# Two attentions and two mixtures of experts on one core: gates spread by DMA, another opening, another order of turns, and split projections

## The chip, the cores and the metric

One core of one Trainium2 chip runs the whole program. The metric is the device time of one execution in microseconds (us). TensorE (PE) multiplies, with its weight loads (PEld) shown apart; VectorE (DVE), ScalarE (ACT) and GpSimd (POOL) do elementwise work; SyncE (SP) only issues DMAs here. DVE, ACT and TensorE reach PSUM, the eight banks of 128x512 floats in which TensorE leaves its products; POOL works on SBUF alone.

## The reference

The input is x, 16 sequences of 256 tokens with 128 features, float32. Four layers follow each other, each of the form x = x + layer(layernorm(x)):

```python
x = x + attn_a(layernorm(x))     # 16 heads of 8; q and k RMS-normed per head; softmax(q k / sqrt 8) v; Wproj, bias
x = x + ffn(layernorm(x))        # 8 experts, top 2 of a softmax gate; plus one shared expert
x = x + attn_b(layernorm(x))     # 16 score heads in 8 pairs, rotary q and k; softmax(2h) - lambda * softmax(2h+1); RMS norm; Wo
x = x + ffn(layernorm(x))        # the same weights again

# ffn, per token: s = softmax(gate(x)), the two largest e
#   out = sum_e  w2[e]( silu((s_e x) w1[e]) * ((s_e x) w3[e]) )  +  w2s( silu(x w1s) * (x w3s) )
```

The gate multiplies x ahead of the expert. So the kernel runs every expert on every token, with x times a gate that is zero where the expert isn't among the two.

## The kernel before

x stays in SBUF for the whole run (`g.x`). Each engine has one instruction stream, written out by `all_steps` (L1649): attention A (`attention_a`), feed-forward f, attention B (`attention_b`), feed-forward h (both `feed_forward`). Within a stream the order is that of the program; engines wait for each other by semaphores (`ev(...)`, `wait_ge`), and an engine that waits holds everything behind it.

**Attentions.** One turn per sequence, 16 turns, each with 16 heads h = 0 to 15 as its clock. The tables `STAGE_A`/`AT_A` and `STAGE_B`/`AT_B` say at which head of which turn a task of a sequence is issued: stage 2 at (7,) is head 7 of the turn two before its own; a number of 16 or more is the next turn. A sequence passes norm, x_turn (transposes into bank XB, L391/L865), a copy to `s_xt` (L488/L990), project (float32 matmuls of x^T with 128x384 weights, L397/L874), the q and k work on DVE and POOL, transposes of k and q through the one bank QK (L338/L769), scores (L354/L787), exp on ACT (L467/L955), values (L368/L819), then o_turn, a_turn, out-projection and residual (L612/L1145). q and k are stored as high and low float32r parts (`split`, `lo`). In A, a Newton iteration of twelve small POOL steps (L522) makes the reciprocal root for the RMS norm.
In B the softmax needs each row's maximum. `maxima` (L804) multiplies q (copied as `s_qp`, L985) with k once, DVE reduces it (L1088, 128x1024 to 128x4, negated) into a spare column of `s_qs`, and then `q_final` transposes q again with this column in it (L769) and ACT copies it to `s_qt` (L976) for the real scores. `s_var` (L1139) and `s_vare` (L1164) are small DVE instructions ahead of POOL's powers (L1045, L1068).

**Feed-forward.** One turn per chunk of 512 tokens, 8 turns, each with nine steps e: eight experts and the shared one (e = 8). At step e TensorE does `up` of expert e+1 (six 128x512 products, L1289 to L1291: three float32r products of high and low parts for w1, three for w3), `spread` of e+3 (L1285), and `down` of e (L1327). The gates of a chunk are computed one chunk ahead, at the steps in `FF` (for the first chunk, inside the last turn of the attention, at `FF_LEAD` steps placed at heads by `LEAD`): norm, x_turn, logits, `best` (maxima, indices, masks), pow on POOL (four pieces, L1444), `gates` (L1535 to L1548). They then reach all partitions through TensorE: `s_turn` transposes them (L1353), ACT copies them (`f_st`, L1414), and `spread` multiplies them with a 0/1 matrix (`g.select`) into the bank SB. DVE's `scale` (L1471) multiplies SB with x^T to `f_xe`, ACT rounds it to `f_xe_hi` (L1403), and the remainder `f_xe_lo` is made by POOL (L1434), or by DVE for the experts in `LOW_ON_DVE` (L1476). DVE's `hidden` (L1487) forms silu(.) times the other product. The order on DVE at step e is: low part of e+2, hidden of e+1, scale of e+3, then the gates' tasks.

**Opening and splits.** `opening` loads x in five parts on SP's queue and the weights on ACT's, and makes the statistics for the first norm. At turn 12 of A, ahead of head 0, DVE makes `w1_hi`, `w3_hi` and `select` (L639 to L641); at turns 13 and 14, ahead of head 0, POOL makes `w1_lo` and `w3_lo` (L503).

## Time and profile before

| | us |
|---|---|
| median of 3 runs | 990.37 (986.24 to 992.31) |
| profiled execution | 989.17, its span 987.4 |
| busy: PE, DVE, ACT, POOL | 874.8, 732.5, 578.9, 528.6 |
| first scores of A | 35.7 |
| first up of f | 255.2 |
| first exp of B | 491.9 |
| first up of h | 767.5 |
| mean granted TensorE clock | 0.973 of full speed |

The span runs from the first to the last instruction of the profiled execution. Busy is the time in which an engine has an instruction under way; a busy TensorE isn't one at its peak, since its matmuls are pipelined. The four firsts divide the span into the opening, A, f, B and h.

### The profile page before, as it was taken

The numbers are of one execution on the slowest core, as the hardware profiler recorded it, in microseconds if no ns is written. First come the engines' busy times: TensorE is split into PE (matmuls) and PEld (weight loads), VectorE is DVE, ScalarE is ACT, GpSimd is POOL, SyncE is SP. The second block draws the span as 40 slices with busy tenths as digits, with TensorE's granted clock in tenths as the row PEclk, the third lists the DMA queues.
The fourth block names the chain that finished last, engine by engine and source line by source line (L and its number), as shares of the span: only waits on it lengthen the run. The fifth ranks groups of instructions, "written<-read, shape, count | busy, mean of one in ns | idle before, by whom it ended". The sixth has DMA issues, their size and how long they took to land.

```text
span 987.4 us, 22246 instructions
## 1 busy us (share of the span) xinstructions
PE 874.8 (89%) x7264; PEld 621.0 (63%) x7264; DVE 732.5 (74%) x1978; ACT 578.9 (59%) x903; POOL 528.6 (54%) x610
## 2 busy tenths in 40 slices
PE   2799999888999999999788888888878799999998
PEld 0355555545688777788555555555545688888887
DVE  4677777766777777777678898989883577767775
ACT  1478778766444434444488888888875344444443
POOL 4666666663444455554436575757542644454551
PEclk9999999988999999999899999999997899999999
DMA  8000000000000000000000000000000000000000
GB/s 235 1 2 1 0 0 0 0 2 2 1 1 1 1 1 0 0 1 1 1 2 1 1 0 0 0 0 0 1 1 1 1 12 12 12 7 4 11 11 23
DMA packets 14607, 8.70 MB, mean 9 GB/s; under 512 B 1616, under 2 KB 14160, under 8 KB 14544
## 3 DMA queue, kind: packets, MB, share of 16 engines
q1 hardware_dynamic: 12960, 7.28, 2.6%
q10 hardware_dynamic: 1584, 0.62, 0.2%
q8 instruction: 35, 0.57, 0.2%
q14 instruction: 28, 0.23, 0.1%
HBM read 5.80 MB, written 2.10 MB: 8 GB/s over the span
## 4 chain that ended last, share of the span: by engine, by line
PE 21%; issue 13%; DVE 11%; POOL 7%; ACT 2%; DVEq 0%; POOLq 0%; ACTq 0%
DVE s_qs L1088 6%; PE psum L819 5%; PE psum L787 5%; POOL f_xe_lo L1434 3%; POOL f_p L1444 3%; PE psum L1327 2%; PE psum L769 2%; PE psum L1289 1%; DVE f_xe L1471 1%; PE psum L885 1%; PE psum L1291 1%; PE psum L1290 1%; PE psum L874 1%; PE psum L804 1%; ACT f_xe_hi L1403 1%
## 5 line engine op out<-in xcount | busy, mean ns | idle before, releaser
L1403 ACT ACTIVATE f_xe_hi<-f_xe 128x512 fp32r<-128x512 f32 x128 | 80.9, 632 | 204.6 <-DVE f_xe L1471 204.6
L1434 POOL TENSOR_TENSOR f_xe_lo<-f_xe,f_xe_hi 128x512 fp32r<-128x512 f32 x64 | 83.9, 1311 | 184.6 <-ACT f_xe_hi L1403 184.6
L1088 DVE TENSOR_REDUCE s_qs<-psum 128x4 fp32r<-128x1024 f32 x128 | 156.3, 1222 | 35.4 <-PE psum L804 34.6
L1327 PEld LDWEIGHTS psum<-w,f_h 128*128 128x128 f32 x1152 | 147.7, 191 | 8.8
L1327 PE MATMUL psum<-w,f_h 128*128 128x128 f32 x1152 | 153.0, 276 | 0.0
L467 ACT ACTIVATE s_probs<-psum 128x1024 f32<-128x1024 f32 x128 | 125.9, 1023 | 33.1 <-PE psum L354 32.7
L955 ACT ACTIVATE s_probs<-psum 128x1024 f32<-128x1024 f32 x128 | 131.3, 1026 | 19.5 <-PE psum L787 17.8
L1289 PE MATMUL psum<-f_xe_hi,w_hi 128*128 128x512 f32 x288 | 127.0, 441 | 7.6 <-POOL f_xe_lo L1434 7.0
L1487 DVE TENSOR_TENSOR f_h<-psum,f_g 128x512 f32<-128x512 f32 x144 | 99.2, 689 | 44.9 <-ACT f_g L1388 34.6
L1291 PE MATMUL psum<-f_xe_lo,w_hi 128*128 128x512 f32 x288 | 114.1, 396 | 0.0
L1290 PE MATMUL psum<-f_xe_hi,w_lo 128*128 128x512 f32 x288 | 113.5, 394 | 0.0
L1471 DVE TENSOR_TENSOR f_xe<-psum,f_xt 128x512 f32<-128x512 f32 x128 | 87.3, 682 | 25.0 <-PE psum L1285 25.0
L1388 ACT ACTIVATE f_g<-psum 128x512 f32<-128x512 f32 x144 | 84.9, 589 | 22.9 <-PE psum L1291 22.5
L1444 POOL TENSOR_TENSOR f_p<-euler,f_sh 128x8 f32<-128x8 f32 x56 | 90.1, 1637 | 1.7
L787 PE MATMUL psum<-s_qt,s_kt 32*128 32x256 f32 x512 | 66.2, 335 | 24.0 <-DVE s_qs L1088 17.3
L787 PEld LDWEIGHTS psum<-s_qt,s_kt 32*128 32x128 f32 x512 | 40.1, 189 | 65.5 <-DVE s_qs L1088 30.4
L1476 DVE TENSOR_TENSOR f_xe_lo<-f_xe,f_xe_hi 128x512 fp32r<-128x512 f32 x64 | 44.4, 694 | 41.4 <-ACT f_xe_hi L1403 41.4
L368 PE MATMUL psum<-s_probs,s_v 128*32 128x256 f32 x1024 | 72.9, 405 | 1.1 <-ACT s_probs L467 1.1
L819 PE MATMUL psum<-s_probs,s_v 128*32 128x256 f32 x1024 | 72.0, 401 | 0.1
L1289 PEld LDWEIGHTS psum<-f_xe_hi,w_hi 128*128 128x128 f32 x288 | 54.4, 189 | 23.9 <-POOL f_xe_lo L1434 10.3
L804 PE MATMUL psum<-s_kt,s_qp 24*128 24x256 f32 x512 | 65.4, 336 | 3.1 <-DVE s_qs L1088 2.1
L1291 PEld LDWEIGHTS psum<-f_xe_lo,w_hi 128*128 128x128 f32 x288 | 54.3, 189 | 12.8
(177 smaller groups left out, 1732.6 us busy)
## 6 DMA issues: line engine op xcount, KB each, us to landing
out<-x SPq DMA_DIRECT2D x8, 256.0 KB, 2.3
x<-in_x SPq DMA_DIRECT2D x3, 512.0 KB, 9.6
w<-in_w SPq DMA_DIRECT2D x3, 512.0 KB, 7.5
x<-in_x SPq DMA_DIRECT2D x2, 256.0 KB, 3.9
select_raw<-in_select SPq DMA_DIRECT2D x1, 512.0 KB, 4.8
rope_cos<-in_rope_cos SPq DMA_DIRECT2D x1, 256.0 KB, 3.9
rope_sin<-in_rope_sin SPq DMA_DIRECT2D x1, 256.0 KB, 4.6
wqkv_a<-in_Wqkv_aT ACTq DMA_DIRECT2D x1, 192.0 KB, 3.6
```

The lines of the kernel that those rows point to most:

```text
L467: act.activation(dst, src, ACT.Exp).then_inc(ex_sb.sem, 1)
L787: ins = pe.matmul(S[:, o:o + SEQ], kt[r:r + 32, k % 2, q, c * P:(c + 1) * P], qt[r:r + 32, k % 2, q, :], start=True, stop=True)
L819: ins = pe.matmul(PV[32 * j:32 * j + 32, :], v1[:, km % 2, c, h // 2, :], probs[:, h % 8, c, :], start=(c == 0), stop=(c == 1))
L955: act.activation(probs[:, 2 * (i % 4):2 * (i % 4) + 2, :, :].rearrange("p j c s -> p (j c s)"), S, ACT.Exp).then_inc(ex_sb.sem, 1)
L1088: dve.tensor_reduce(o[:, r:r + 2, 2 * p:2 * p + 2, 24:25].bitcast(F32R), room(km, i).rearrange("p (r j s) -> p r j s", r=2, j=2), AX.X, AL ...
L1289: pe.matmul(dst, w_hi, x_hi, start=True, stop=False)
L1290: pe.matmul(dst, w_lo, x_hi, start=False, stop=False)
L1291: return pe.matmul(dst, w_hi, x_lo, start=False, stop=True)
L1327: ins = pe.matmul(Y[k % 2][:, t * P:(t + 1) * P], g.f_h[:, q, t * P:(t + 1) * P], g.w2[:, e, :], start=(e == 0 and t == 0), stop=(e == NE ...
L1434: pool.tensor_tensor(xe_lo[:, ring(e), :], src, xe_hi[:, ring(e), :], ALU.subtract).then_inc(xe_lo_pool.sem, 1)
L1444: pool.tensor_tensor(g.f_p[:, i * w:(i + 1) * w], g.euler[:, 0:w], g.f_sh[:, i * w:(i + 1) * w], ALU.pow).then_inc(pw_sb.sem, 1)
L1487: dve.tensor_tensor(g.f_h[:, q, :], H3[q], g.f_g[:, q, :], ALU.mult).then_inc(h_sb.sem, 1)
```

## The change

It has five parts.

1. **Gates by DMA.** The spreading through TensorE is gone. DVE transposes the gates in 32x32 blocks (`f_sg`), SP writes them to a DRAM tensor and reads each expert's row back, broadcast over the 128 partitions, into one of four buffers `f_gt`. `scale` multiplies that buffer with x^T.
2. **The feed-forward's order.** The gates' tasks of a chunk are issued two chunks ahead and spread over more steps (`FF`); `LOW_ON_DVE` goes from (2, 5, 6, 7) to (2, 3); the shared expert's parts are made at step 2; `LEAD` places the first chunk's tasks one or two heads earlier.
3. **Projections.** In both attentions the float32 projection becomes three float32r products of high and low parts. ACT makes `x_hi`, DVE `x_lo` (task `xl`), and the weights are split once.
4. **Attention B.** q is transposed and copied once, for maxima and scores alike. The maxima go to a tensor of their own (`s_mxs`), TensorE transposes them to 16 rows (`max_turn`), ACT copies these, and a DMA on SP writes them into the spare rows of `s_qt`. Two small instructions move from DVE to POOL, some tasks move by a head.
5. **Opening and splits.** x is loaded in eight parts, of which SP issues four ahead of the weights' arrival; statistics, roots and sequence 1's tasks have other places (`EARLY_A`); sequences 0 and 1 use more banks; sequence 0's Newton steps run on DVE; the splits of w1 and w3 stand at heads 11 and 5 instead of ahead of head 0.

```diff
-PARTS = ((0, 4), (4, 8), (8, 16), (16, 24), (24, 32))
-STATISTICS = ((-3, 0), (-2, 11), (-1, 12), (0, 8), (0, 12))
-ROOTS = ((-3, 0), (-2, 15), (-1, 15), (0, 15), (1, 5))
+PARTS = tuple((t, t + 4) for t in range(0, NT, 4))
+LOADED = ((0, 1), (1, 1), (2, 2), (2, 2), (3, 4), (3, 4), (3, 4), (3, 4))
+STATISTICS = {(-3, 0): (0,), (-3, 12): (1,), (-1, 8): (2,), (-1, 12): (3,), (0, 4): (4,), (0, 11): (5,), (1, 4): (6,), (1, 9): (7,)}
+ROOTS = {(-3, 0): (0,), (-2, 5): (1,), (-1, 13): (2, 3), (0, 14): (4, 5), (1, 14): (6, 7)}
...
+            if i == 4:
+                sp.wait_ge(first_loaded, first_count)
+            sp.dma_start(g.x[:, lo:hi, :], x_view[:, lo:hi, :]).then_inc(x_loaded[LOADED[i][0]], 16)
...
+                act.wait_ge(first_loaded, first_count)
+                act.activation(g.wqkv_a_hi[:], g.wqkv_a[:], ACT.Copy).then_inc(w_split, 1)
...
+NEWTON_ON_DVE = 1
+EARLY_A = {(1, "norm", 0): (-3, 11), (1, "xt", 0): (-2, 5), (1, "xt_keep", 0): (-2, 8), (1, "xl", 0): (-2, 8), (1, "qkv", 0): (-2, 9),
+           (1, "qkv", 1): (-2, 10), (1, "square", 0): (-2, 12), (1, "sums", 0): (-1, 3), (1, "newton", 0): (-1, 4)}
...
+    def room(m, c):
+
+        return bank(3) if m < 2 and c == 1 else XB
+
+    def turned(m, i):
+
+        return bank((5, 0, 1, 2)[i]) if m == 0 else QK
...
-                pe.wait_ge(qkv_sb.sem, qkv_sb.upto(m, c))
-                pe.matmul(XB[:, 0:3 * P], xt[:, c * P:(c + 1) * P], wqkv[:],
-                          start=True, stop=True).then_inc(qkv_mm.sem, 1)
+                if km >= 2:
+                    pe.wait_ge(qkv_sb.sem, qkv_sb.upto(m, c))
+                dst, c = room(km, c)[:, 0:3 * P], slice(c * P, (c + 1) * P)
+                pe.matmul(dst, x_hi[:, c], w_hi[:], start=True, stop=False)
+                pe.matmul(dst, x_hi[:, c], w_lo[:], start=False, stop=False)
+                pe.matmul(dst, x_lo[:, c], w_hi[:], start=False, stop=True).then_inc(qkv_mm.sem, 1)
...
-            if k in (13, 14):
-
-                pool.wait_ge(g.late_loaded, g.late_count)
-                pool.wait_ge(w_hi_sb.sem, k - 12)
-                w, hi, lo = ((g.w1, g.w1_hi, g.w1_lo), (g.w3, g.w3_hi, g.w3_lo))[k - 13]
-                pool.tensor_tensor(lo[:], w[:], hi[:], ALU.subtract)
             for h in part:
+                if k in (13, 14) and h == 5:
+
+                    pool.wait_ge(w_hi_sb.sem, k - 12)
+                    if k == 13:
+                        pool.tensor_tensor(g.wqkv_b_lo[:], g.wqkv_b[:], g.wqkv_b_hi[:], ALU.subtract)
+                    w, hi, lo = ((g.w1, g.w1_hi, g.w1_lo), (g.w3, g.w3_hi, g.w3_lo))[k - 13]
+                    pool.tensor_tensor(lo[:], w[:], hi[:], ALU.subtract)
...
+                if k in (12, 13) and h == 11:
+
+                    dve.wait_ge(g.late_loaded, g.late_count)
+                    if k == 12:
+                        dve.tensor_scalar(g.wo[:], g.wo[:], 4 * (1.0 - LAMBDA_INIT), None, ALU.mult)
+                    if k == 12:
+                        dve.tensor_copy(g.wqkv_b_hi[:], g.wqkv_b[:])
+                    w, hi = ((g.w1, g.w1_hi), (g.w3, g.w3_hi))[k - 12]
+                    dve.tensor_copy(hi[:], w[:]).then_inc(w_hi_sb.sem, 1)
...
+                for off in due("xl", 0, h, k):
+
+                    m = n + off
+                    dve.wait_ge(xt_sb.sem, xt_sb.upto(m, 1))
+                    dve.tensor_tensor(x_lo[:], XB[:, 0:SEQ], x_hi[:], ALU.subtract).then_inc(xt_sb.sem, 1)
...
-    "pv": 5, "norm": (9,), "xt": (3,), "qkv": (6, 10), "rot": (13,), "sum": (0,), "split": (6, 1), "lo": (7, 2),
-    "kt": (8, 19), "qp": (11, 16), "max": tuple(range(14, 30, 2)), "qf": (7, 15), "v": (4,),
-    "otr": (2, 4), "tokens": (2, 4), "diff": (6,), "sq2": (6,), "mean": (7,), "pow": (8,), "head": (8,), "atr": (12,),
+    "pv": 5, "norm": (9,), "xt": (3,), "xl": (4,), "qkv": (6, 10), "rot": (13,), "sum": (0,), "split": (6, 1), "lo": (7, 2),
+    "kt": (7, 19), "qp": (11, 15), "max": tuple(range(14, 30, 2)), "mt": (8, 16), "v": (4,),
+    "otr": (3, 5), "tokens": (3, 5), "diff": (6,), "sq2": (6,), "mean": (7,), "pow": (8,), "head": (8,), "atr": (13,),
...
+            def max_turn(m, km, p):
 
                 pe.wait_ge(mx_sb.sem, mx_sb.upto(m, 4 * p + 4))
-                if p == 0:
+                if km + 1 < NSEQ:
+                    if p == 0:
+                        pe.wait_ge(kt_sb.sem, kt_sb.upto(m + 1, 1))
+                    else:
+                        pe.wait_ge(qp_sb.sem, qp_sb.upto(m + 1))
+                elif p == 0:
                     pe.wait_ge(kt_sb.sem, kt_sb.upto(m))
-                elif km + 1 < NSEQ:
-                    pe.wait_ge(qp_sb.sem, qp_sb.upto(m + 1, 1))
                 else:
-                    pe.wait_ge(qf_sb.sem, qf_sb.upto(m, 1))
-                turn(qs[:, km % 2], p).then_inc(qf_mm.sem, 1)
+                    pe.wait_ge(mt_sb.sem, mt_sb.upto(m, 1))
+                pe.transpose(QK[0:16, 0:P], mxs[:, km % 2, p].rearrange("p r j c -> p (r j c)"),
+                             g.identity[:]).then_inc(mt_mm.sem, 1)
...
+                        act.activation(mt[0:16, p, :], QK[0:16, 0:P], ACT.Copy).then_inc(mt_sb.sem, 1)
...
+                    pool.wait_ge(ms_sb.sem, ms_sb.upto(m))
+                    pool.tensor_tensor(g.s_var2[:], g.s_ms2[:], g.rms_eps[:], ALU.add).then_inc(var_sb.sem, 1)
...
+        for m in range(NSEQ):
+            n = Step(None, 0, m)
+            for p in range(2):
+                sp.wait_ge(mt_sb.sem, mt_sb.upto(n, p + 1))
+                sp.dma_start(qt[24:P:32, m % 2, 2 * p:2 * p + 2, :].rearrange("r j (c t) -> r (j c) t", c=2).bitcast(F32),
+                             mt[0:16, p, :].bitcast(F32)).then_inc(row_sb[p].sem, 16)
...
-LOW_ON_DVE = (2, 5, 6, 7)
+LOW_ON_DVE = (2, 3)
+LOW_ON_POOL = (0, 1, 4, 5, 8, 6, 7)
+HIGH_ORDER = (0, 1, 2, 3, 4, 5, 8, 6, 7)
...
-LEAD = {1: (0,), 3: (1,), 4: (2,), 6: (3,), 8: (4,), 9: (5,), 13: (6,), 15: (7,)}
+LEAD = {0: (0,), 2: (1,), 3: (2,), 5: (3,), 6: (4,), 7: (5,), 13: (6,), 15: (7,)}
...
-    "norm": 8, "x_turn": 0, "xt_sb": 0, "logits": 1, "best": 1, "pow": (2, 2, 2, 2), "gates": 5, "s_turn": 6,
-    "st_sb": 6, "residual": 0, "rstd": 0,
+    "norm": 4, "x_turn": 5, "xt_sb": 5, "logits": 6, "best": 7, "masks": 8, "pow": 7, "sums": 2, "gates": 3,
+    "residual": 5, "stats": 6, "rstd": 8, "shared": 2,
 }
-FF_LEAD = {"x_turn": 0, "xt_sb": 1, "logits": 2, "best": 2, "exp": 4, "gates": 5, "s_turn": 6, "st_sb": 6}
+FF_LEAD = {"x_turn": 0, "xt_sb": 1, "logits": 2, "best": 2, "masks": 2, "exp": 4, "sums": 5, "gates": 5}
...
-            def spread(m, km, e):
-
-                if e == 0:
-                    if km == 0:
-
-                        pe.wait_ge(before.turned.sem, before.turned.upto(last))
-                    pe.wait_ge(st_sb.sem, st_sb.upto(m))
-                    pe.wait_ge(xe_sb.sem, xe_sb.upto(m - 1))
-                else:
-                    pe.wait_ge(xe_sb.sem, xe_sb.upto(m, e))
-                pe.matmul(SB, g.select[:, e, :], st[:, km % 2, :],
-                          start=True, stop=True).then_inc(sb_mm.sem, 1)
...
-                dve.tensor_tensor(xe[:, e % 2, :], SB, xt[:, km % 2, :], ALU.mult).then_inc(xe_sb.sem, 1)
+                dve.tensor_tensor(xe[:, e % 2, :], gt[:, e % 4, :], xt[:, km % 2, :], ALU.mult).then_inc(xe_sb.sem, 1)
...
-                dve.wait_ge(st_mm.sem, st_mm.upto(n))
-                dve.tensor_copy(ssp[:, :, 0:E].bitcast(F32R), g.f_m[:, 0, :, :]).then_inc(hi_sb.sem, 1)
-                dve.wait_ge(hi_sb.sem, hi_sb.upto(n + 1))
-                dve.tensor_tensor(ssp[:, :, E:2 * E], g.f_m[:, 0, :, :], ssp[:, :, 0:E], ALU.subtract).then_inc(lo_sb.sem, 1)
+                dve.wait_ge(sc_sb.sem, sc_sb.upto(m))
+                dve.wait_ge(written.sem, written.upto(m - 1))
+                dve.transpose(g.f_sg[:], g.f_m[:, 0, :, :].rearrange("p t e -> p (t e)")).then_inc(sg_sb.sem, 1)
...
+        for m in range(NCH):
+            n = Step(None, 0, m)
+            sp.wait_ge(sg_sb.sem, sg_sb.upto(n))
+            sp.dma_start(g.gates[m % 2].rearrange("e (t b j) -> b (e t) j", t=4, b=4),
+                         g.f_sg[:]).then_inc(written.sem, 16)
+            sp.wait_ge(written.sem, written.upto(n))
+            for e in range(E):
+                if e >= 4 or m > 0:
+                    sp.wait_ge(xe_sb.sem, xe_sb.upto(n, e - 3) if e >= 4 else xe_sb.upto(n - 1, e + 5))
+                sp.dma_start(gt[:, e % 4, :], g.gates[m % 2, e].partition_broadcast(P)).then_inc(gt_sb[e % 4].sem, 16)
+                if not first and e == 3 and m >= 2:
+                    store(m - 2)
```

## Rows read from the trace of the kernel before

**Rows 1.** Windows (A, feed-forward, two B turns): us, busy PE PEld DVE ACT POOL, clock, DMA.

```profile
122.76:135.33 12.57, 12.11 (x140) 6.88 (x132) 9.56 (x32) 10.07 (x14) 8.52 (x18) 1.00 0.00 0
342.77:369.40 26.63, 25.22 (x147) 21.06 (x146) 20.17 (x64) 11.42 (x20) 14.00 (x10) 1.00 0.00 1
620.34:654.17 33.83, 30.00 (x345) 18.23 (x346) 30.54 (x59) 28.54 (x47) 21.54 (x21) 1.00 0.00 0
```

**Rows 2.** Waits of TensorE's weight loads, 314.5 to 447.7; total us, times, longest.

```profile
PEld psum L1353 <- DVE f_ss L1548: 6.2, 5, 1.3
PEld psum L1285 <- DVE f_xe L1471: 3.1, 5, 0.8
PEld psum L1289 <- POOL f_xe_lo L1434: 2.7, 5, 0.6
```

**Rows 3.** Timeline of one expert's step; start, duration (us), engine, line, what.

```profile
338.66 0.40 PE L1285 MATMUL psum<-f_st,select 128*128 128x512 f32 x1
338.89 1.05 PE L1327 MATMUL psum<-w,f_h 128*128 128x128 f32 x8
339.80 0.51 PE L1289 MATMUL psum<-f_xe_hi,w_hi 128*128 128x512 f32 x1
341.31 0.39 PE L1285 MATMUL psum<-f_st,select 128*128 128x512 f32 x1
342.18 0.68 DVE L1471 TENSOR_TENSOR f_xe<-psum,f_xt 128x512 f32<-128x512 f32 x1
343.60 1.29 POOL L1434 TENSOR_TENSOR f_xe_lo<-f_xe,f_xe_hi 128x512 fp32r<-128x512 f32 x1 [3.85 <-ACT f_xe_hi L1403]
```

**Rows 4.** Timeline, two-input instructions of DVE and POOL at once, feed-forward.

```profile
347.23 1.28 POOL L1434 TENSOR_TENSOR f_xe_lo<-f_xe,f_xe_hi 128x512 fp32r<-128x512 f32 x1 [0.92 <-ACT f_xe_hi L1403]
347.60 0.96 DVE L1520 TENSOR_TENSOR f_sh<-f_lg,f_top 128x32 f32<-128x32 f32 x1
348.64 6.44 POOL L1444 TENSOR_TENSOR f_p<-euler,f_sh 128x8 f32<-128x8 f32 x4
351.20 0.69 DVE L1476 TENSOR_TENSOR f_xe_lo<-f_xe,f_xe_hi 128x512 fp32r<-128x512 f32 x1 [0.70 <-ACT f_xe_hi L1403]
```

**Rows 5.** DMA issues; count, KB each, us from issue to landing.

```profile
out<-x SPq DMA_DIRECT2D x8, 256.0 KB, 2.3
bqkv<-in_bqkv ACTq DMA_DIRECT2D x1, 192.0 KB, 6.7
```

**Rows 6.** Timeline of attention B, two small DVE instructions.

```profile
601.19 0.47 DVE L1139 TENSOR_SCALAR s_var<-s_ms 128x16 f32<-128x16 f32 x1
606.55 1.28 POOL L1061 TENSOR_TENSOR s_rot<-s_qkv,rope_sin 128x512 f32<-128x512 f32 x1
606.72 1.13 DVE L1164 TENSOR_SCALAR s_vare<-s_mv 128x2 f32<-128x2 f32 x1
607.84 1.22 DVE L1088 TENSOR_REDUCE s_qs<-psum 128x4 fp32r<-128x1024 f32 x1
```

**Rows 7.** Timeline of attention A: a projection; two residuals; the weight split.

```profile
120.03 0.91 PE L397 MATMUL psum<-wqkv_a,s_xt 128*128 128x384 f32 x2
191.28 0.41 DVE L612 TENSOR_TENSOR x<-psum,x 128x256 f32 x1
223.48 0.41 DVE L612 TENSOR_TENSOR x<-psum,x 128x256 f32<-128x256 f32 x1
209.70 2.62 POOL L503 TENSOR_TENSOR w_lo<-w,w_hi 128x1152 fp32r<-128x1152 f32 x1
209.74 2.87 DVE L577 CAST s_qs<-s_qh 128x512 fp32r<-128x512 f32 x1
```

**Rows 8.** Timeline of the opening.

```profile
17.52 0.29 POOL L522 TENSOR_TENSOR s_yt<-s_y 128x64 f32<-128x64 f32 x1 [10.48 <-DVE s_y L594]
22.42 1.07 POOL L530 TENSOR_TENSOR s_qh<-s_qkv,s_y 128x512 f32<-128x512 f32 x1 [0.23 <-POOL s_y L522]
35.70 0.80 PE L354 MATMUL psum<-s_qt,s_kt 32*128 32x256 f32 x8 [1.18 <-DVE s_qt L668]
```

372 lines of the change are left out of this document (194 added, 178 removed).

## The prediction

> **What bounds the kernel now.** I read the views in the order of the work. The busy time per turn comes first [rows 1]: each row is a steady stretch, one turn of attention A (12.57 us), one of the feed-forward (26.63 us), two of attention B (33.83 us, 16.92 each). In the feed-forward TensorE is busy 25.22 of 26.63 us and DVE 20.17: TensorE is the bound, with some waits. In A it is 12.11 of 12.57. In B DVE (30.54 of 33.83) and TensorE (30.00) are equally full, so there the two hand work to each other and neither is the bound alone.
>
> Next the waits of TensorE's weight loads over five feed-forward turns [rows 2]: 6.2 us for `f_ss` (the transpose of the gates), 3.1 us for `f_xe` (the spreading matmul waits until DVE has emptied its bank), 2.7 us for POOL's `f_xe_lo`. That is 1.24, 0.62 and 0.54 us a turn. The first two belong to instructions that the change deletes.
>
> Then one expert's step in the timeline [rows 3]: spread at 338.66, down matmuls at 338.89, the next up matmuls at 339.80. The six up matmuls end with the next spread's start at 341.31. So a spread takes 0.23 us, a down 0.91 and an up 1.51; the later `f_xe` of 342.18 and `f_xe_lo` of 343.60 show a second ring, priced below.
>
> **The feed-forward, 16 turns.** Deleted from TensorE in each: 8 spreads x 0.23 = 1.83 us, and the gate transpose, four 128x128 matmuls, 0.46 us (half of the eight in a down). Their waits go too, 1.24 + 0.62. Were nothing late next, a turn would be 26.63 - 4.15 = 22.5 us.
> Something is late next: the ring that feeds x. From an up's start (339.80) DVE multiplies its product (hidden), then gates x for two experts later (342.18), ACT rounds it, POOL subtracts (343.60 + 1.29 = 344.89) [rows 3]. That is 5.09 us, about 5.15 with the signal, and the up two steps later needs it. Two of TensorE's new steps are only 2 x (1.51 + 0.91) = 4.8 us; the spreads covered the rest. POOL now makes six of the eight gated low parts in place of four (experts 0, 1, 4 to 7). Walking the nine steps with 2.40 us each, at least 5.15 from the up two before to every up that needs a POOL low part (a DVE low part is 0.6 shorter and binds nothing), and x_turn (0.46, as half a down) and the logits (0.91, eight small loads as a down) at steps 5 and 6, gives 24.1 us a turn. Without the ring it is 9 x 2.40 + 1.37 = 23.0, which is also what 25.22 busy less 2.29 leaves.
> DVE loses two low parts of 0.69 and two casts and gains one 32x32 transpose: about -1.6 us, from 20.17 to 18.6. But the gating product changes its operands from PSUM and SBUF to SBUF and SBUF. The rows show what that risks: at 347.60 a 128x32 tensor_tensor with both operands in SBUF takes 0.96 us, ending when POOL's pass (347.23 + 1.28) ends; at 351.20 one of 128x512 takes 0.69 us in the midst of POOL's four pow (348.64 + 6.44) [rows 4]. So POOL's subtraction holds DVE up and its pow does not. The new products start about 0.35 us before POOL's previous pass ends, at this step length; on five pairs that makes 24.7, if none of it is caught up. I take 24.2, nearer the ring alone since DVE may reorder its slack, a gain of 2.45 us x 16 = 39 us (first and last turns of a layer lose their gates' work too, some of it outside the turn). Bounds: 22.9 (no ring, 60 us) and 25.5 (18 us, most of a POOL pass waited for at each product).
> The Trainium skill, "SBUF — State Buffer", section "Who interferes with whom", says that a DVE instruction with two SBUF inputs contends with any GpSimd instruction that reads SBUF, the later one fully blocked. Read to the letter the pow blocks too; the 0.69 us inside the pow speaks against that much. By the rule the turn would be that of the second rival.
> New waits: the gates go by DMA to DRAM and back. The gates are ready three steps before the first product, 3 x 2.5 = 7.5 us. The nearest transfers land 2.3 us after issue (256 KB to DRAM) and 6.7 us (a 192 KB row spread over partitions, among many others) [rows 5]. Two transfers: 4.6 us at best, 13.4 at worst; I take 6, hidden. The other broadcasts have four buffers, so 10 us each, and SP has no other work but the stores. Queued behind a late one on DVE are hidden(8), the statistics and the next products. The pow of POOL (6.44) moves to where POOL has no low part for three steps; cover 7.3 us. Pieces of the statistics and masks only change their step: nothing, as DVE has 5 us free; if that cover goes, 2 us a turn.
>
> **Attention B, 16 turns.** Right before the max reduction of 607.84 [rows 6] DVE sits in `s_vare`, 1.13 us for 128x2, which ends with POOL's pass (606.55 + 1.28). It and `s_var` (0.47 at 601.19) go to POOL: DVE -1.6, +0.41 for the new low part of x (as the 0.41 of [rows 7]), net -1.2. TensorE loses eight transposes (0.91, as a down), gains two (0.23), and each projection falls from 0.91 [rows 7] to three products of 384 columns, 3 x 0.17 + 0.17 of tail = 0.69: together -1.1. ACT, busy in 28.54 of 33.83, loses two 128x512 copies and gains two small ones. The row DMAs have eight heads (8 us) before their use, against 2.3 to 6.7: hidden. Because DVE and TensorE alternate, only what lies between two reductions counts: I see 0.5 us at s_vare, about 0.45 at the others. 0.95 x 16 = 15 us. Bounds: nothing (the small steps fill up again with the new DVE step and the later o_turn) and 2.0 a turn, 32 us.
>
> **Attention A, 16 turns.** Projections -0.22 x 2. But DVE now makes x_lo at the head of the turn, after the statistics of the residual, and the first projection waits for it: +0.3. Net -0.1 x 16 = 2 us; bounds -5 and +3.
>
> **The weight splits.** The two turns from 191.28 to 223.48 take 32.20 us against 2 x 12.57: 7.06 too long, and the turn after meets the second POOL pass, another 3. The reason stands at 209.70: POOL's `w_lo` (2.62 us) starts and DVE's cast of 209.74 takes 2.87 us [rows 7], with TensorE empty behind it. The change puts the DVE casts at head 11, the POOL passes at head 5, ahead of the wait for the Newton seed (POOL is busy in 8.52 of 12.57 us [rows 1]), and drops select. One DVE copy (v) still meets them. I take 7 of the 10 us back; bounds 3 and 10.
>
> **The opening.** First scores are at 35.70. Newton on POOL runs from 17.52 to 22.2 [rows 8]: twelve steps of 0.39. On DVE a step of 128x256 takes 0.41 [rows 7]; for 128x64 I estimate 0.22: -2. The two projections no longer wait for each other's addition (-2), the four turns of sequence 0 have a bank each instead of one (-3.5), x is normalised before the weights land (-1), and sequence 1 is taken out of its way. Added: split of the weights, some 1.5 us, beside the transposes. Sum -9; bounds -5 and -12.
>
> **The hand-overs.** Gates for the first chunk take 6 us by DMA instead of a transpose, a copy and a spread (0.46, some 0.6 and 0.23, with the signals 2 us), but are asked for two heads (some 2 us) earlier and the last exps hold the first up in any case; a pow of 6.44 us earlier on POOL. +1; bounds -3 and +6.
>
> **Sum.** -39 - 15 - 2 - 7 - 9 + 1 = -71 us. The profiled execution took 989.17 us (span 987.4), which is 1.2 below the median of the three runs, 990.37; so 918 to 919. I say 919.
>
> **Rivals.**
> TensorE floor. The ring is slack because DVE gets ahead within the turn; turns of 22.9. For it: no wait on POOL's part exceeds 0.6 today [rows 2]. Against: such waits exist although spreads slow the pace. 919 - 21 = 898. Chance 0.17.
> DVE locked out. Every gating product waits for a POOL pass as the 0.96 us one did, 0.8 x 8 = 6.4 us on an engine with 18.6: 25 and more, a turn of about 26; FF gains 10 in place of 39: 948. For it: [rows 4]. Against: the pow row, and that the products start late in the pass. Chance 0.15.
> B does not move: its turn stays 16.92 as the ring re-forms; 934. Chance 0.07, inside the range.
> Slower: gates late. If write and broadcast take together over 9 us, DVE's first product, and behind it hidden(8), hold TensorE, microsecond for microsecond. At the worst end, 13.4 plus 2 us of issue and a queue of four broadcasts (2 us more), a turn is 24.2 + 8.4 = 32.6 and 14 such turns cost 118 us: 1037. It is slower than before from a chain of 14 us (71 / 14 = 5 us over 9). Against: 2.3 us for a whole 256 KB store. Chance 0.05.
> Nothing: the gains are given back to within 1%, 0.03 (by a mixture of the lower bounds: 18 + 0 - 3 + 3 + 5 - 6 = 17 us, 972).
>
> **Numbers.** The forecast itself (905 to 935) has 0.53. The range takes in the floor rival and the locked one, 892 to 948; outside are the late gates, nothing, and the ends of the two. A measurement of this kernel tells about 1% from no change. Faster 0.92, same 0.03, slower 0.05.
>
> **What would show it.** Right: no PE wait before the feed-forward's transpose of the gates, turns of 24.2, waits on `f_xe_lo` of 1 to 2 us a turn, gating products of 0.69 to 1.05 us; B turns near 16.0 with s_vare gone from DVE; A turns 12.5; first scores at 26 to 27; a turn 13 to 15 of A under 14 us. Wrong: products of over 1.3 us, DVE waiting for `f_gt`, B at 16.9, or the copies of v holding A for 3 us.

## The result: no gain, and the profile after

The changed kernel took 991.76 us (median of 20 runs), the kernel before 988.78 in the same comparison: ratio 1.0029, 95% interval 1.0015 to 1.0042. The forecast was 919. The profiled execution took 989.9 us with a span of 988.0 (before 989.17 and 987.4). The interval lies just above 1: the changed kernel is 0.3% slower, and all of the 71 us of forecast gain is absent.

Stage by stage, from the starts of the same instructions in both traces (A's and B's residuals, the hidden products of the two feed-forward layers f and h):

| stretch | before | after | change | forecast |
|---|---|---|---|---|
| start to A's first residual | 66.4 | 59.9 | -6.5 | -9 |
| (first scores at) | 35.70 | 32.26 | -3.4 | 26 to 27 |
| ten turns of A | 124.9 | 126.2 | +1.3 | -1 |
| three turns of A with the weight splits | 45.1 | 38.3 | -6.7 | -7 |
| A's 14th residual to f's first hidden | 21.5 | 24.1 | +2.5 | hand-overs +1 in all |
| seven turns of f | 189.6 | 191.7 | +2.1 | -17 |
| f's last turn to B's first residual | 76.8 | 82.8 | +6.0 | |
| eleven turns of B | 186.2 | 178.1 | -8.1 | -10 |
| B's 12th residual to h's first hidden | 59.5 | 66.2 | +6.7 | |
| h and the end | 217.4 | 220.7 | +3.3 | -20 |

(The forecast's 39 us of the feed-forward are spread over 16 turns here, its 15 of B over 16. A hand-over is the stretch in which one layer's last turn and the next layer's first overlap: three rows, from A's 14th residual, from f's last turn and from B's 12th residual.) Attention behaved; the feed-forward, expected to give 39, lost 5, and the hand-overs lost 15.

The busy time of steady stretches, as [rows 1]: two turns of A, one of f, two of B; columns as there, and GB/s last.

```profile
110.08:135.44 25.36, 23.67 (x269) 14.55 (x268) 18.91 (x65) 19.81 (x26) 17.15 (x37) 1.00 0.00 0
350.22:378.17 27.95, 23.80 (x138) 19.98 (x138) 21.33 (x63) 10.65 (x19) 16.83 (x13) 1.00 0.23 76
619.92:652.26 32.34, 28.22 (x336) 17.56 (x336) 29.21 (x57) 27.24 (x47) 22.16 (x25) 1.00 0.00 1
```

TensorE was in fact relieved in the feed-forward, from 25.22 us a turn [rows 1] to 23.80, and the turn is longer. So something else set its length. The waits of five turns of f, as [rows 2] (total, times, longest):

```profile
ACT f_xe_hi L1458 <- DVE f_xe L1520: 75.6, 40, 2.8
POOL f_xe_lo L1484 <- ACT f_xe_hi L1458: 55.8, 26, 3.8
DVE f_h L1536 <- ACT f_g L1443: 25.7, 21, 1.4
PEld psum L1361 <- POOL f_xe_lo L1484: 22.2, 24, 1.5
```

The waits for `f_ss` (6.2) and for the spread bank (3.1) are gone, and the wait for POOL's low part has gone from 2.7 to 22.2. One expert's step shows how the work runs in a circle, as [rows 3]:

```profile
361.70 0.68 DVE L1536 TENSOR_TENSOR f_h<-psum,f_g 128x512 f32<-128x512 f32 x1
362.31 0.68 DVE L1520 TENSOR_TENSOR f_xe<-f_gt,f_xt 128x512 f32<-128x512 f32 x1
363.10 0.63 ACT L1458 ACTIVATE f_xe_hi<-f_xe 128x512 fp32r<-128x512 f32 x1 [1.82 <-DVE f_xe L1520]
363.64 0.58 ACT L1443 ACTIVATE f_g<-psum 128x512 f32<-128x512 f32 x1
364.37 0.68 DVE L1536 TENSOR_TENSOR f_h<-psum,f_g 128x512 f32<-128x512 f32 x1
364.97 0.68 DVE L1520 TENSOR_TENSOR f_xe<-f_gt,f_xt 128x512 f32<-128x512 f32 x1
```

Gating product, its rounding, the silu queued behind the rounding on ACT, the hidden product, and on DVE behind it the next gating product: 362.31 to 364.97, 2.66 us, with no matmul in it (DVE also makes a low part in this step). The same circle ran before the change, 339.52 to the `f_xe` of 342.18 [rows 3], 2.66 us too; these are its lines between, which the prediction did not look at:

```profile
339.52 0.68 DVE L1471 TENSOR_TENSOR f_xe<-psum,f_xt 128x512 f32<-128x512 f32 x1
340.24 0.63 ACT L1403 ACTIVATE f_xe_hi<-f_xe 128x512 fp32r<-128x512 f32 x1 [1.47 <-DVE f_xe L1471]
340.81 0.60 ACT L1388 ACTIVATE f_g<-psum 128x512 f32<-128x512 f32 x1
341.57 0.69 DVE L1487 TENSOR_TENSOR f_h<-psum,f_g 128x512 f32<-128x512 f32 x1
```

Before the change 48 of 106 steps of steady turns, hidden product to hidden product, last 2.55 to 2.63 us, most of them 2.59; after it only 25 of 106 do, other short ones last 2.46 or 2.64. The long ones, up to 4.7 us, hold the places where DVE and POOL meet, as [rows 4]:

```profile
366.89 1.26 POOL L1484 TENSOR_TENSOR f_xe_lo<-f_xe,f_xe_hi 128x512 fp32r<-128x512 f32 x1
367.44 1.26 DVE L1520 TENSOR_TENSOR f_xe<-f_gt,f_xt 128x512 f32<-128x512 f32 x1
371.02 1.50 DVE L1520 TENSOR_TENSOR f_xe<-f_gt,f_xt 128x512 f32<-128x512 f32 x1
373.12 2.06 DVE L1548 TENSOR_SCALAR f_xn<-x,mean,rstd 128x128 f32 x4
373.26 1.33 POOL L1484 TENSOR_TENSOR f_xe_lo<-f_xe,f_xe_hi 128x512 fp32r<-128x512 f32 x1 [1.29 <-ACT f_xe_hi L1458]
374.64 0.50 PE L1361 MATMUL psum<-f_xe_hi,w_hi 128*128 128x512 f32 x1 [1.31 <-POOL f_xe_lo L1484]
```

Gating products of 1.26 and 1.50 us instead of 0.68, and a normalisation of 2.06 that takes 1.11 in the kernel before (337.50). The hidden product (375.10) stands behind the normalisation; TensorE's up of 374.64 waits for the low part of 373.26, which is late because the product of 371.02 is.

### The profile page after: what moved, and what is told of

Read it like the earlier page. It is cut to its first block, busy times and chain, and to the rows that moved or that the text cites. A ratio compares the mean times of both kernels' runs of the same rounds, so it can differ in the third digit from the quotient of the medians.

```text
span 988.0 us, 21977 instructions
## 1 busy us (share of the span) xinstructions
PE 834.2 (84%) x7040; PEld 600.9 (61%) x7040; DVE 724.2 (73%) x1949; ACT 556.2 (56%) x889; POOL 577.3 (58%) x668
## 4 chain that ended last, share of the span: by engine, by line
POOL 15%; PE 14%; DVE 13%; issue 9%; ACT 2%; POOLq 0%; DVEq 0%; ACTq 0%
DVE s_mxs L1156 7%; POOL f_xe_lo L1484 4%; POOL s_inv L1110 3%; POOL f_p L1496 2%; PE psum L874 2%; PE psum L842 2%; PE psum L1399 2%; PE psum L1361 2%; POOL s_qh L1084 1%; POOL s_rot L1125 1%; POOL s_rot L1126 1%; PE psum L1362 1%; PE psum L1363 1%; DVE f_xe L1520 1%; DVE s_qs L1183 1%
## 5 line engine op out<-in xcount | busy, mean ns | idle before, releaser
L1484 POOL TENSOR_TENSOR f_xe_lo<-f_xe,f_xe_hi 128x512 fp32r<-128x512 f32 x96 | 122.3, 1275 | 194.0 <-ACT f_xe_hi L1458 194.0
L1156 DVE TENSOR_REDUCE s_mxs<-psum 128x4 fp32r<-128x1024 f32 x128 | 155.9, 1219 | 29.1 <-PE psum L859 27.8
L1361 PE MATMUL psum<-f_xe_hi,w_hi 128*128 128x512 f32 x288 | 129.5, 450 | 51.4 <-POOL f_xe_lo L1484 46.9
L1399 PEld LDWEIGHTS psum<-w,f_h 128*128 128x128 f32 x1152 | 150.5, 193 | 10.9
L1520 DVE TENSOR_TENSOR f_xe<-f_gt,f_xt 128x512 f32<-128x512 f32 x128 | 103.9, 812 | 4.3 <-DMA f_gt<-gates 4.3
L1361 PEld LDWEIGHTS psum<-f_xe_hi,w_hi 128*128 128x128 f32 x288 | 54.8, 190 | 79.2 <-POOL f_xe_lo L1484 59.5
L842 PE MATMUL psum<-s_qt,s_kt 32*128 32x256 f32 x512 | 68.4, 345 | 37.6 <-DVE s_mxs L1156 35.2
L1496 POOL TENSOR_TENSOR f_p<-euler,f_sh 128x8 f32<-128x8 f32 x56 | 95.4, 1729 | 1.8
L874 PE MATMUL psum<-s_probs,s_v 128*32 128x256 f32 x1024 | 75.7, 417 | 0.0
L400 PE MATMUL psum<-s_probs,s_v 128*32 128x256 f32 x1024 | 72.1, 401 | 1.3 <-ACT s_probs L503 1.3
L859 PE MATMUL psum<-s_kt,s_qt 24*128 24x256 f32 x512 | 67.7, 343 | 3.6 <-DVE s_mxs L1156 2.7
L1362 PEld LDWEIGHTS psum<-f_xe_hi,w_lo 128*128 128x128 f32 x288 | 55.1, 191 | 6.5
```

Source lines behind the costliest of these rows:

```text
L842: ins = pe.matmul(S[:, o:o + SEQ], kt[r:r + 32, k % 2, q, c * P:(c + 1) * P], qt[r:r + 32, k % 2, q, :], start=True, stop=True)
L1156: dve.tensor_reduce(mxs[:, km % 2, p, r:r + 2, :, c:c + 1].bitcast(F32R), room(km, i).rearrange("p (r j s) -> p r j s", r=2, j=2), AX.X, A ...
L1361: pe.matmul(dst, w_hi, x_hi, start=True, stop=False)
L1362: pe.matmul(dst, w_lo, x_hi, start=False, stop=False)
L1399: ins = pe.matmul(Y[k % 2][:, t * P:(t + 1) * P], g.f_h[:, q, t * P:(t + 1) * P], g.w2[:, e, :], start=(e == 0 and t == 0), stop=(e == NE ...
L1484: pool.tensor_tensor(xe_lo[:, ring(e), :], src, xe_hi[:, ring(e), :], ALU.subtract).then_inc(xe_lo_pool.sem, 1)
```

## The experiments

Two theories on the feed-forward. **S (step ring):** the 2.59 us circle above sets the short steps, before and after, because of DVE's order; TensorE was not the bound. **L (lock):** POOL's subtraction shuts out DVE's instructions with both operands in SBUF, and some with one there (the normalisation above); the change made the gating product one of the first and gave POOL six gated low parts instead of four. Rivals: **C**, the chain of low parts through POOL is long by itself; and my own reading, TensorE. The table has the turn (mean of five in f, five in h, from one profiled execution each) and the whole kernel against the kernel before of the same chip. Excerpts of code leave out the semaphores' waits and marks.

| kernel | f turn | h turn | us | ratio (95%) |
|---|---|---|---|---|
| before | 27.22 | 26.64 | | |
| changed | 27.61 | 26.97 | 991.76 | 1.0029 (1.0015 to 1.0042) |
| e1, no subtraction on POOL | 25.44 | 24.78 | 969.46 | 0.982 (0.979 to 0.986) |
| e2, product ahead of hidden | 24.28 | 23.50 | 942.47 | 0.956 (0.952 to 0.959) |
| e3, x from PSUM | 26.62 | 26.39 | 979.90 | 0.993 (0.991 to 0.995) |
| e4, e2 + e3 | 23.49 | 22.44 | 926.28 | 0.937 (0.934 to 0.940) |
| e5, before with tiny spreads | 26.99 | 26.41 | 984.69 | 0.998 (0.996 to 1.001) |
| e6, before with e2's order | 25.56 | 25.55 | 972.88 | 0.984 (0.981 to 0.987) |
| e15, e1 + e2 | 24.30 | 23.21 | 940.45 | 0.952 (0.948 to 0.956) |

**e1.** The lock alone.

```diff
-pool.tensor_tensor(xe_lo[:, ring(e), :], src, xe_hi[:, ring(e), :], ALU.subtract)
+pool.tensor_tensor(xe_lo[:, ring(e), 0:6], g.euler[:, 0:6], g.minus_half[:, 0:6], ALU.pow)
...
+if k == 13: pool.memset(g.f_xe_lo[:].bitcast(F32), 0.0)      # once, in attention A
```

> Changed kernel, but GpSimd's low part in the feed-forward is a power of 128x6 elements (estimated from 1.00 us for 128x4 and 1.73 us for 128x8: 1.3 us) instead of the subtraction of 128x512 (1.28 us): the same wait, the same place, nearly the same time, but almost nothing read from SBUF. Left out: the low parts of the gated input. Theory L (lock): VectorE's gating product, with both operands in SBUF since the change, is shut out while GpSimd subtracts; then the products are all 0.69 us (now 0.69 to 1.50), and the feed-forward turn falls from 27.8/27.0 to 23.5 to 24.5 us, the kernel by 45 to 55 us to 935 to 945. Rival C (chain): the turn is long because six instead of four low parts go through GpSimd, 1.3 us each in the chain product, high, low, up; then the turn stays within 0.5 us of 27.8/27.0 and the kernel at 980 or above.

All 128 products took 0.68 to 0.72 us, though POOL was as busy (1.32 us for each stand-in). The turn fell by 2.2 us in both layers, not by 3 to 4, and the kernel came to 969, above the 935 to 945 expected. L is real and C as the whole cause falls, but it gives back 20 to 22 us of the kernel, under a third of what was missing. Some 3 us of that comparison are the edit's own: the memset takes 2.23 us of POOL (204.98) in the three turns with the weight splits, which last 41.3 us against 38.3.

**e2.** The ring alone: one pair of lines of DVE's order.

```diff
+for m, km, next_e in ahead(n, k, e, 3):
+    if next_e < E: scale(m, km, next_e)
 for m, km, next_e in ahead(n, k, e, 1):
     hidden(m, km, next_e)
-for m, km, next_e in ahead(n, k, e, 3):
-    if next_e < E: scale(m, km, next_e)
```

> Changed kernel, VectorE's order in a feed-forward step turned round: the gating product for three steps ahead before the hidden product. Theory S (step ring): most steps, before and after the change, last 2.59 us because the silu on ScalarE stands behind the rounding of the next product, that waits for the product, that stands on VectorE behind the hidden product, that waits for the silu before: 0.69 + 0.63 + 0.58 + 0.69. Then the short steps fall from 2.59 to 2.3 to 2.45 us (TensorE's own work), and if the lock of theory L is what is left in the long ones, the turn goes from 27.8/27.0 to 25 to 26.5. Rival: the short steps are TensorE's own length; they stay at 2.59 and the turn stays or grows, since the hidden product comes later.

The turn fell by 3.3 and 3.5 us, more than expected, and the kernel by 4.4% against the one before, 4.7% against the changed one. Of the 106 steps only 4 still last 2.55 to 2.63 us; short ones are 2.0 to 2.5. Nothing was taken away from any engine, and the gating products are not shorter for it (0.85 us in the mean in f, 0.91 in h). So DVE's order is the cause of 3.3 to 3.5 us a turn. That the circle of 2.59 us is all that it does is not shown: after the change part of the gain lies in the step behind the longest one, 2.46 us before and 1.26 now, where TensorE seems to catch up on what it had waited for.

**e3 and e4.** The product's x from the PSUM bank that the spread had used, for six of eight turns in a layer (one ACT copy of 128x512 a turn); e4 has e2's order too.

```diff
+if 2 <= k + 1 < NCH and e == 5:
+    act.activation(X, xt[:, (k + 1) % 2, :], ACT.Copy).then_inc(xp_sb.sem, 1)
...
-dve.tensor_tensor(xe[:, e % 2, :], gt[:, e % 4, :], xt[:, km % 2, :], ALU.mult)
+dve.tensor_tensor(xe[:, e % 2, :], gt[:, e % 4, :], X if km >= 2 else xt[:, km % 2, :], ALU.mult)
```

> Changed kernel, with the transposed x for the gating products held in the PSUM bank that the change freed (one ScalarE copy of 128x512 a turn, some 0.6 us, for six of eight turns of a layer): the product reads SBUF and PSUM as it did before the change. Output complete. Theory L: the products are 0.68 us in these turns, the turn falls to 24.5 to 26 (the normalisation and two low parts on VectorE still meet GpSimd), the kernel to 955 to 970. Rival C: products shorten but the turn stays within 0.5 of 27.8/27.0.

> e3 and e2 together. If L and S both hold, the two causes are separate and their gains add: turns of 23 to 24.5 us, the kernel at 935 to 955. If only L holds: as e3. If neither: near 988.

In e3 the products of these turns are 0.67 to 0.68 us, and the turn is 1.0 and 0.6 us shorter, less than half of e1's gain. The rest of the lock is on DVE's small instructions, which e1 freed and e3 did not: in the mean an `f_xn` takes 0.52 us in the changed kernel and in e3, 0.35 in e1; `f_sh` 0.85, 0.85 and 0.17; `f_vare` 0.65, 0.65 and 0.17. DVE's own low parts take 0.69 in all three. e3 missed its range (980 against 955 to 970). e4 went beyond its own, turns of 23.49 and 22.44 against 23 to 24.5 and 926 us against 935 to 955, and took what e2 and e3 gave apart (4.3 and 4.1 us a turn summed, 4.1 and 4.5 together). Four of its turns in the view of busy time (PE, PEld, DVE, ACT, POOL):

```profile
794.55:883.15 88.60, 88.60 (x555) 78.46 (x554) 70.23 (x197) 46.62 (x80) 61.34 (x45) 1.00 0.33 108
```

TensorE is busy in 88.60 of 88.60 us, and neither its matmuls nor its weight loads stand in the list of waits of this stretch. Here it is the bound, as I had thought it was before the change: 22.15 us a turn is what its work comes to.

**e5 and e6.** The same question put to the kernel before, from both sides.

```diff
+w = CH if km == 0 else 32
-pe.matmul(SB, g.select[:, e, :], st[:, km % 2, :], start=True, stop=True)
+pe.matmul(SB[:, 0:w], g.select[:, e, :], st[:, km % 2, 0:w], start=True, stop=True)
```

> Kernel before, but the spreading matmul of every chunk after a layer's first writes 32 columns instead of 512: TensorE is relieved of some 0.2 us x 8 a turn and nothing else is touched (the gates of the rest of the columns are left out). The prediction held TensorE to be the feed-forward's bound (25.22 us busy of 26.63): then the turn falls by 1.5 to 1.8 us and the kernel by 20 to 25 us. Theory S (the step of 2.59 us is a ring of VectorE and ScalarE: product, high part, silu, hidden, and the next product) says that TensorE was not the bound: the turn falls by less than 0.5 us, the kernel by less than 8.

> Kernel before, with the gating product ahead of the hidden product in each step of VectorE's order, as in e2. Theory S: the ring is opened, and TensorE becomes the bound: 25.2 us of its work in a turn and some waits, so 25.5 to 26.3 instead of 26.7 us a turn, the kernel 6 to 18 us faster. If TensorE was the bound already: no change (within 4 us).

Relieving TensorE of its spreads moved the turn by 0.23 us in both layers and the kernel by less than it can be measured. In e5 the steps of 2.59 us stayed (47 of 106 in 2.55 to 2.63). Turning DVE's order round moved the turn by 1.7 and 1.1 us and left none of them, and only then did TensorE's spreads bind: DVE's idle time before the gating products that ended with the spreading matmul rose to 74.7 us over the kernel, from 25.0:

```profile
  PE psum L1285: 25.0, 15
```

```profile
  PE psum L1285: 74.7, 84
```

(Kernel before, then e6: total us, times.) Both came out as theory S had it. This is the plainest answer to the prediction: the spreads, the largest part of what the change deletes, were not in the way.

**e15.** Both causes away.

> e1 and e2 together: GpSimd's low parts as a power of the same length that does not shut VectorE out, and the gating product ahead of the hidden one. Left out: the low parts of the gated input that GpSimd makes. With neither the lock nor the step ring, TensorE is left: 8 x 6 up and 32 + 4 down matmuls and the transposes and logits of the gates, as e4 shows in the second layer, so 22.1 us a turn there (26.97 in the changed kernel, 24.78 with the ring alone, 23.50 with the lock alone). Rival, a third limit in the low parts' chain through GpSimd (six of 1.3 us and 6.6 us of power a turn): above 23.

23.21 in h, not 22.1, and 24.30 in f, which is e2's 24.28: the rival's condition (above 23) is met, and the gains of e1 and e2 do not add. TensorE's weight loads wait for POOL's part again (4.6 us, four times, from 794 to 883), which in e4 they never do there. POOL's power for the gates took 1.87 us a piece in the median against 1.64 in e4, and its stand-in 1.35 in the mean against 1.29 for the subtraction there. The values are not the reason, for e2, with the real ones, has 1.91. Every piece over 1.7 us, in all kernels, ran while a DVE tensor_tensor with both operands in SBUF was under way: 48 of 56 pieces in e2, 11 in e4, none in the kernel before, whose product reads PSUM. So with x in SBUF the lock also works the other way: the product holds POOL's power up, by as much as 0.5 us, though the power does not hold the product up (52 products beside a power alone took 0.67 to 0.70 us in e2). POOL's chain is then the next limit, within 1 us of TensorE's. (e15 has e1's memset too, and 42.4 us in the turns with the weight splits against 38.3.)

**e8.** The gates' way over DRAM.

```diff
-sp.wait_ge(sg_sb.sem, sg_sb.upto(n))
-sp.dma_start(g.gates[m % 2].rearrange(...), g.f_sg[:]).then_inc(written.sem, 16)
-sp.wait_ge(written.sem, written.upto(n))
...
-sp.dma_start(gt[:, e % 4, :], g.gates[m % 2, e].partition_broadcast(P))
+sp.dma_start(gt[:, e % 4, :], g.row[e].partition_broadcast(P))
```

> Changed kernel with the broadcasts of the gates read from a constant table in DRAM, with no write of the gates and no wait for it (the gates are left out of the result; all of VectorE's work for them stays). It prices the latency of the gates' way. Theory: in the steady turns nothing waits for it (no wait on f_gt is seen), so 27.8/27.0 stays within 0.3; at the hand-overs VectorE waited 4.3 us for the first chunk's gates (753.69 to 758.03 in B's end), so 3 to 8 us come back in both together. Rival: the traffic itself (16 broadcasts of 256 KB a turn stay) or nothing: no change at all.

27.57 and 27.01 a turn, the kernel 991.67 (0.49% above the one before, 0.29% for the changed one): the latency costs nothing that shows. The wait of 4.3 us that DVE has in B's end is gone there, and the stretch from B's 12th residual is no shorter (67.0 us against 66.2). The stretch from A's 14th residual is shorter (20.8 us against 24.1), but no wait for the gates stood in it, and e8 has the full clock all through it, while the others with the same code there have 3.4 to 10.2 us at 1.2 GHz and take 22.1 to 24.1 us. Right about the turns, wrong about the hand-overs.

**e7.** The projections.

```diff
-pe.matmul(dst, x_hi[:, c], w_hi[:], start=True, stop=False)
-pe.matmul(dst, x_hi[:, c], w_lo[:], start=False, stop=False)
-pe.matmul(dst, x_lo[:, c], w_hi[:], start=False, stop=True)
+pe.matmul(dst, x_hi[:, c], w_hi[:], start=True, stop=True)      # x_hi, w_hi: the whole float32 here
```

> Changed kernel with both attentions' projections as one float32 product of x and the weights again (the low part of x is not made; the splits of the weights stay). The prediction gave -0.1 us a turn of A (12.4/12.95 now) and some 0.44 + 0.4 us of TensorE and VectorE a turn of B (16.17 now) to the three products. If that was right: B turns 16.3 to 16.6, A turns within 0.2. Rival: the low part of x on VectorE is a new wait (A: the first projection waits for it; the hand-over from the feed-forward to B: TensorE waited 4.29 us for it at 465.23): then A turns fall by 0.2 to 0.4 us, B does not grow, and the stretch from the feed-forward's turn 7 to B's first residual (82.8 us, 76.8 before) falls by 3 to 5 us.

The rival, nearly on every count. A's turn falls from 12.62 to 12.46 (0.2 to 0.4 was expected), B's from 16.20 to 16.11, and from f's last turn to B's first residual it takes 78.6 us instead of 82.8. The first scores come at 29.51 instead of 32.26, but A's first residual no earlier (59.8 against 59.9). The changed kernel's wait there:

```profile
464.75 0.42 DVE L1240 TENSOR_TENSOR s_x_lo<-psum,s_x_hi 128x256 fp32r<-128x256 f32 x1
465.23 0.44 PE L935 MATMUL psum<-wqkv_b_hi,s_x_hi 128*128 128x384 f32 x1 [4.29 <-DVE s_x_lo L1240]
466.06 0.49 ACT L1060 ACTIVATE s_qkv<-psum 128x384 f32<-128x384 f32 x1 [6.09 <-PE psum L937]
466.53 0.77 PE L1361 MATMUL psum<-f_xe_hi,w_hi 128*128 128x512 f32 x1
```

`s_x_lo` stands on DVE behind the layer's statistics and a cast that waits for POOL's rotation; the projection waits for it, and the feed-forward's next up matmuls stand behind the projection. But the kernel gained little (984.93, ratio 0.995, 0.992 to 0.999): it lost 2.1 us in the turns with the weight splits and 2.0 before h's first hidden product, where its clock was the lowest of all (next table).

**e9.** Attention B's last turns.

```diff
-turn(qs[:, km % 2], p).then_inc(qp_mm.sem, 1)
+for _ in range(2 if k >= 12 else 1): ins = turn(qs[:, km % 2], p)
+ins.then_inc(qp_mm.sem, 1)
... (the same for K's and the outputs' transposes)
```

> Changed kernel; in attention B's turns 12 to 15 TensorE makes the transposes of K, Q and the outputs twice (the same result, some 3.6 us more work a turn, into banks that are its own at that time). After the change TensorE has less work there and the trace shows its granted clock at 0.5 from 711.7 us on (before the change from 738): from the 11th residual to the next layer's first hidden product 66.2 us against 59.5. Theory K: the loss is the clock, which falls because TensorE idles more between the max reductions; then the clock stays at 1.0 longer and the stretch falls by 2 to 7 us in spite of the added work. Rival: the stretch is long for what stands in it (the gates' new place, the waits); then it grows by 1 to 6 us.

The views of busy time of the kernel before, the changed kernel and e9, same times (the third number from the end is the granted clock; the 12th residual stands at 710.45, 701.08 and 702.58, so the kernel before is 9 us behind in its work):

```profile
708.00:714.00 6.00, 5.17 (x67) 3.42 (x60) 5.10 (x11) 4.87 (x8) 3.98 (x5) 1.00 0.01 3
732.00:738.00 6.00, 4.60 (x64) 2.64 (x64) 4.95 (x8) 4.37 (x7) 3.13 (x3) 1.00 0.00 0
```

```profile
708.00:714.00 6.00, 3.94 (x45) 2.25 (x42) 4.98 (x9) 4.27 (x7) 5.07 (x5) 0.80 0.00 1
732.00:738.00 6.00, 5.57 (x38) 3.29 (x38) 2.63 (x11) 2.81 (x4) 1.35 (x3) 0.50 0.00 1
```

```profile
708.00:714.00 6.00, 4.83 (x61) 2.98 (x53) 5.51 (x9) 4.32 (x8) 2.72 (x5) 1.00 0.00 0
732.00:738.00 6.00, 4.03 (x42) 2.51 (x43) 4.32 (x14) 4.32 (x6) 2.62 (x4) 1.00 0.01 3
```

With more to do TensorE keeps 2.4 GHz until 742, and the stretch to h's first hidden takes 63.9 us instead of 66.2, though it holds more work (turns 13 and 14 are 17.2 and 16.4 us against 18.2 and 18.3; the turn before them, also with doubled transposes, is 1.0 longer). One execution each could be chance, but other kernels bear it out: e1, e3 and e8 have nearly the changed kernel's code in this stretch, and their clocks differ.

| from B's 12th residual to h's first hidden | us at 1.2 GHz | us |
|---|---|---|
| kernel before | 17.1 | 59.5 |
| e9, doubled transposes | 20.5 | 63.9 |
| changed | 37.5 | 66.2 |
| e3, same code here | 37.5 | 66.2 |
| e8, same code here but for the gates' way | 41.0 | 67.0 |
| e1, same code here but for POOL's low parts | 44.4 | 67.7 |
| e7, single products | 47.8 | 68.3 |

The length follows the clock: 0.16 us for each us at 1.2 GHz by a line through the last six rows, 0.22 by one through the four that are neither e9 nor e7. Brought to the 17 us of the kernel before, the changed kernel would have 62 to 63. That is an estimate of 3 to 4.5 us for the clock out of the 6.7 lost, of which e9 shows 2.4. When the clock falls is not the change's doing alone: in e8 it stayed full until 726.9, in the changed kernel until 711.7. The kernel as a whole did not gain by e9 (988.11, ratio 1.000, 0.998 to 1.003, against 1.003, 1.002 to 1.004, of the changed one).

**e10.** Two edits in different stages.

```diff
+dve.tensor_scalar(g.s_var2[:], g.s_ms2[:], 16 * RMS_EPS_B, None, ALU.add)
+dve.tensor_scalar(g.s_vare[:], g.s_mv[:, 0:2, 1], LN_EPS, None, ALU.add)
-pool.tensor_tensor(g.s_var2[:], ...); pool.tensor_tensor(g.s_vare[:], ...)
...
-EARLY_A = {(1, "norm", 0): (-3, 11), ..., (1, "qkv", 0): (-2, 9), ..., (1, "newton", 0): (-1, 4)}
+EARLY_A = {(1, "norm", 0): (-3, 11), (1, "xt", 0): ..., (1, "xt_keep", 0): ..., (1, "xl", 0): ...}
```

> Changed kernel with two edits in stages that don't meet. Attention B: the additions for s_var and s_vare go back to VectorE. The prediction gave 0.5 of the 0.75 us that a turn lost to taking s_vare away: turn from 16.20 to 16.6 to 16.9. Rival: the turn got shorter by the deleted turns of the q bound and the moved steps; then within 0.15 of 16.20. Opening: sequence 1's projections, squares and Newton steps at their ordinary heads instead of early ones. In the trace of the changed kernel VectorE adds sequence 1's bias (21.78, 22.74) while sequence 0's q and k (ready on GpSimd at 20.5) wait for their casts at 23.21: theory Q: first scores at 28.5 to 30.5 instead of 32.3. Rival: sequence 1 is then late and what is gained is given back by attention A's first residual (59.9).

B's turn is 17.16 us, above the 16.6 to 16.9 expected, so these two additions are worth 0.96 a turn, all of B's gain and more: without them the changed B is 0.24 slower than the one before (16.92). The wait of [rows 6] is back, an addition that ends with POOL's pass, right ahead of a max reduction:

```profile
589.42 1.29 POOL L1123 TENSOR_TENSOR s_rot<-s_qkv,rope_sin 128x512 f32<-128x512 f32 x1
589.60 1.13 DVE L1225 TENSOR_SCALAR s_vare<-s_mv 128x2 f32<-128x2 f32 x1
590.71 1.21 DVE L1151 TENSOR_REDUCE s_mxs<-psum 128x4 fp32r<-128x1024 f32 x1
```

The opening moved by 0.5 us only (first scores 31.73; 32.2 to 32.8 in the nine kernels with the changed opening): theory Q was largely wrong. The whole kernel took 1002.44 (1.017, 1.011 to 1.023).

**e11 to e14.** Towards a better kernel. e11 and e12 keep the hidden product first in the lead; e13 and e14 don't; e12 to e14 have e7's single products; e14 has e9's transposes.

```diff
+for go in first_hidden + first_scale if k == -1 else first_scale + first_hidden:
+    go()
```

> e4 (transposed x in PSUM, gating product first), but in a layer's lead, before its first turn, the hidden product stays first. In e4 the first hidden product came 3.7 us later than in the changed kernel, with a first turn 3.8 us shorter. Expected: first hidden product back at 248.5, the first turn 0 to 4 us longer; the kernel 0 to 6 us below e4's 926.

> e11 with the projections of both attentions as one float32 product, as in e7. If the low part of x in the hand-over is a cost of its own (4.2 us in e7 between the feed-forward's turn 7 and B's first residual) and the rest of e7 holds here, 4 to 8 us below e11. If e7's gains are taken back by later stretches as they were there (3.7 us at the end): 0 to 4.

> e4 (transposed x in PSUM, gating product first also in the lead) with the projections as one float32 product. e12 took 11 us off e11; if the low part of x in the hand-overs is what it removes, the same holds here: 926 - 11 = 915, between 912 and 920. If e12's gain hung on the lead's order: 920 to 926.

> e13 with the doubled transposes of e9 in attention B's turns 12 to 15. If the clock's early fall costs there what it cost in the changed kernel (e9: 63.9 instead of 66.2 us in the stretch), 1 to 4 us below e13; if the second transposes only fill TensorE: 1 to 4 above.

e11: 930.45 (0.942, 0.938 to 0.947), no better than e4, where 0 to 6 us less were expected. e12: 919.56 (0.933, 0.928 to 0.938), 11 us below e11 instead of 4 to 8. e13: 920.33 (0.931, 0.928 to 0.934), 6 us below e4 and just above its 912 to 920, so e12's gain hung in part on the lead's order. e12, e13 and e14 can't be told apart; they are the best measured, 6.7 to 6.9% under the kernel before, and e13's interval just touches e4's (0.934 to 0.940). e14: 922.22 (0.933, 0.931 to 0.936): its profiled execution was 4.6 us shorter than e13's, but its median was not.

## Why the prediction was wrong, step by step

- **The bound.** "TensorE is the bound, with some waits" was read from 25.22 busy of 26.63 us. e5 disproves it. A busy share of 95% did not make it the bound. The 2.59 us circle of DVE and ACT lies as near as can be to TensorE's own step, for which the prediction added up 2.65; that sum is too long, since steps of 2.59 were seen beside it. With the circle opened and the spreads kept (e6) the turn is 25.6, so TensorE would have been the next bound, 1.1 to 1.7 us lower. This is the step that failed first: from here the forecast subtracted 4.15 us of TensorE's work and waits, of which e5 takes away some 1.6 (from a spread's start to the next matmul's 0.03 us instead of 0.23, eight times) and gets 0.23.
- **The ring that feeds x.** I walked one ring (up, hidden, product, high, low, up two steps later) at an assumed step of 2.40 and missed the shorter one through the order of two queues: ACT has the silu behind the next rounding, DVE has the next product behind the hidden one. 0.68 + 0.63 + 0.60 + 0.69 from [rows 3] and its neighbours is 2.60 a step, nine steps 23.4 us before anything else is late. By e2 DVE's order is worth 3.3 to 3.5 us a turn with the lock in place, and 47 us of the kernel by the two ratios (0.956 against 1.003), more than the 39 forecast.
- **The lock.** The rows were seen and priced for the gating products alone, and the value taken (24.2) leaned on "DVE may reorder its slack", which no row showed. Over five turns of h the products average 0.79 us, over five of f 0.86, so 0.9 and 1.4 us a turn where the step from 24.1 to 24.7 had put 0.6: not five of them late by 0.35, but the sixth and seventh of a turn by up to 0.83. By e1 the whole lock is 2.2, since the normalisations, `f_vare` and `f_sh` meet POOL's passes too (`f_sh` did before the change as well, 0.84). The rival "DVE locked out" had the nearest turn (about 26) for half of the reason. Its time, 948, was also too low. One of the prediction's own signs of being wrong, products of over 1.3 us, is there in 18 of 128.
- The Trainium skill, "SBUF — State Buffer", section "Who interferes with whom", has both halves: two SBUF inputs contend with a GpSimd instruction that reads SBUF, and tensor_scalar in its two-port mode too; the traces agree for the subtraction (0.68 to 1.50, 1.11 to 2.06). They do not for the power: in e1 POOL's 112 stand-ins read SBUF and none of 128 products passed 0.72 us, while the power itself was held up beside such products (1.64 to as much as 2.18 us in e2).
- **B.** -0.72 us a turn against -0.95: right in size, partly wrong in reason. s_vare and s_var gave 0.96 (e10) where I had 0.5; the three products, counted as part of a 1.1 us relief, cost 0.09 (e7).
- **A.** +0.13 a turn, forecast -0.1, within its bounds; the products cost 0.16 (e7), because x_lo stands ahead of the first projection on DVE, as feared.
- **The weight splits.** -6.7 against -7. Right, by the mechanism given.
- **The opening.** -6.5 at the first residual against -9, first scores at 32.26 against 26 to 27. By e7 the split of x and weights takes 2.7 us of the first scores, where I had hidden 1.5 "beside the transposes", and nothing of the first residual. What the rest of the missing 5 to 6 us is stays open. "Sequence 1 is taken out of its way" was the reverse of what the trace shows (its bias additions stand at 21.78 and 22.74 ahead of sequence 0's cast at 23.21), but e10 prices that at 0.5 only.
- **Gates by DMA.** Hidden, as said: DVE's only wait for `f_gt` in the profiled execution is the 4.3 us in B's end, and e8 shows that to be worth nothing. The rival of late gates did not happen.
- **The hand-overs.** +1 became +15. 4.2 are the new wait for x_lo (e7; 3.3 by e13 against e4, whose clocks in the stretch are alike). At least 2.4, by estimate 3 to 4.5, are the clock in B's last turns. The other two stretches hold 3.4 and 6.8 us more at 1.2 GHz than before, by the same estimate some 2 us together. What the other 5 or so are stays open.
- **The outcome.** "Nothing" had a chance of 0.03, as a mixture of every term's lower bound (972 by its own sum, which is not within 1% either). That is not how it came: the feed-forward, bounded at 18 us gained, lost 5, the hand-overs passed their +6 by 9, and B and the splits came in near their forecast.

## What to carry to other kernels

Before an engine is called the bound, follow the queue order of the others for one step and add up any circle that closes without it; where two have the same length, taking work off one gives nothing until the order that makes the other is changed (here two exchanged loops, worth 1.6% before the change and 4.7% after it). When a change turns an operand from PSUM into SBUF, or gives POOL more passes, price every instruction of both engines that will now meet, in both directions, not the changed one alone. And a split into high and low parts is a step on VectorE that others stand behind: at a hand-over it cost more than its three products saved.

## Not expected of the hardware

- In e10's and the unchanged B an addition of 128x2 elements takes 1.13 us, since it ends when POOL's 128x512 pass does; as a POOL instruction it takes 0.19 us (its fellow of 128x16 0.22) and costs DVE nothing.
- POOL's power took 1.64 us for 128x8 in the median and up to 2.17 in the changed kernel, and 1.91 in the median in e2, where DVE's gating product runs beside it more often; in the kernel before, never more than 1.64.
- TensorE's granted clock fell to 1.2 GHz in B's last turns 28 us earlier after the change than before it (711.7 against 740.0), and doubled transposes held it at 2.4 GHz until 742.4: a kernel with more matmuls was no slower. Where it falls differs between kernels with the same code there (726.9 in e8), so one execution's stretch with a low clock can't be compared with another's before the clocks are.
